# Row-maximum scores of two units written to two neighbouring banks, with one maximum instruction over 1024 columns

## The reference, cut to what matters

```python
scores = jnp.einsum('bhqd,bhkd->bhqk', q, k) * scale + mask
a = jax.nn.softmax(scores, axis=-1)
```

## Time and profile before

| | |
|---|---|
| median of 3 executions | 1685.04 us (1684.78 to 1686.82) |
| the profiled execution's own time | 1684.44 us |
| its span, first to last instruction | 1682.7 us |
| DVE busy | 1244.4 us in 3785 instructions |
| of that, the row maxima (line 881) | 516.8 us in 768 instructions |
| mean granted TensorE clock | 0.96 of full speed |

### The profile page before, as it was taken

How to read it: one execution, slowest core, us unless ns; L and a number is a source line. 1 busy time by engine, 2 the same in 40 slices (tenths; PEclk the granted TensorE clock), 3 DMA queues, 4 the chain that set the end, 5 groups by cost and what they waited for, 6 DMA issues and landing times.

```text
span 1682.7 us, 39867 instructions
## 1 busy us (share of the span) xinstructions
PE 1513.9 (90%) x13672; PEld 1095.7 (65%) x13672; DVE 1244.4 (74%) x3785; ACT 914.0 (54%) x1919; POOL 725.6 (43%) x1097
## 2 busy tenths in 40 slices
PE   5569999999999999999999999999999872999993
PEld 3346776676766767777777777766777552777772
DVE  2346888888888878878888888888887742688883
ACT  1235666666666666666666666666666542222220
POOL 1111444444444444444444444444444333366666
PEclk8789999999999999999999999999999985999997
DMA  4997466766666666666666566666666302355540
GB/s 108 191 201 140 83 106 107 107 104 102 103 100 100 101 103 103 101 101 104 98 104 105 103 105 103 103 104 106 102 97 96 93 27 88 104 163 178 175 133 11
DMA packets 253512, 183.56 MB, mean 109 GB/s; under 512 B 29284, under 2 KB 251943, under 8 KB 253310
## 3 DMA queue, kind: packets, MB, share of 16 engines
q1 hardware_dynamic: 244126, 176.22, 57.5%
q0 software_dynamic: 6912, 3.73, 0.8%
q10 hardware_dynamic: 2272, 1.06, 0.3%
HBM read 55.78 MB, written 38.04 MB: 56 GB/s over the span
## 4 chain that ended last, share of the span: by engine, by line
PE 64%; POOL 11%; DVE 9%; issue 8%; SPq 5%; DMA 1%; ACTq 1%; ACT 1%; POOLq 0%; DVEq 0%
PE bank L1242 13%; PE bank L1389 8%; PE bank L1348 7%; PE bank L1224 4%; SPq L406 4%; PE bank L1232 4%; PE bank L1273 4%; PE bank L1270 3%; PE bank L1211 3%; DVE bst L817 3%; POOL rstd L526 3%; PE bank L1203 3%; PE bank L1199 3%; POOL slots_scratch L581 2%; POOL xrow L592 2%
## 5 line engine op out<-in xcount | busy, mean ns | idle before, releaser
L881 DVE TENSOR_REDUCE mx<-bank 128x2 f32<-128x512 f32 (+1 forms) x768 | 516.8, 674 | 170.3 <-PE bank L1270 90.2
L667 ACT ACTIVATE pt<-bank 128x512 f32<-128x512 f32 x768 | 450.7, 594 | 295.4 <-PE bank L1211 171.0
L1242 PE MATMUL bank<-xnT,weff 128*128 128x256 f32 x1024 | 257.8, 396 | 13.8 <-DVE rest L865 13.1
L1242 PEld LDWEIGHTS bank<-xnT,weff 128*128 128x128 f32 x1024 | 188.7, 194 | 50.2 <-DVE rest L865 15.3
L1273 PE MATMUL bank<-stack 96*128 96x256 bf16 x1024 | 197.7, 275 | 5.6 <-DVE mx L881 5.3
L1211 PE MATMUL bank<-stack 100*128 100x128 bf16 x2048 | 198.8, 219 | 0.0
L548 POOL TENSOR_TENSOR parts<-rest,parts 128x512 bf16<-128x512 f32 x128 | 147.1, 1159 | 115.4 <-ACT parts L684 115.4
L678 ACT ACTIVATE parts<-bank,bqk 128x256 bf16<-128x256 f32 x256 | 107.5, 471 | 136.4 <-PE bank L1242 126.2
L559 POOL TENSOR_TENSOR obuf<-obuf,xrow 128x512 f32<-128x512 f32 x32 | 40.6, 1270 | 326.4 <-ACT obuf L709 326.4
L1211 PEld LDWEIGHTS bank<-stack 100*128 100x128 bf16 x2048 | 158.6, 97 | 12.9
L1208 PE MATMUL bank<-tri,identb 128*128 128x256 bf16 x512 | 141.0, 275 | 20.0 <-DMA stack<-mT 18.2
(11 more groups left out here) (152 smaller groups left out, 2754.9 us busy)
## 6 DMA issues: line engine op xcount, KB each, us to landing
stack<-parts SPq DMA_DIRECT2D x384, 128.0 KB, 5.9
stack<-parts SPq DMA_DIRECT2D x768, 64.0 KB, 2.6
slots_scratch<-zeros SPq DMA_DIRECT2D x5, 2080.0 KB, 12.5
xr<-x SPq DMA_DIRECT2D x32, 256.0 KB, 8.7
out<-obuf SPq DMA_DIRECT2D x32, 256.0 KB, 2.2
ew<-w_gate SPq DMA_DIRECT2D x32, 256.0 KB, 4.0
ew<-w_up SPq DMA_DIRECT2D x32, 256.0 KB, 5.2
ew<-w_down SPq DMA_DIRECT2D x32, 256.0 KB, 4.4
```

The source lines that it names most:

```text
L667: act.activation(pt[:, u % 8, :], S2[u % 2][:, :], ACT.Exp).then_inc(p_ready, 1)
L881: dve.reduce_max(dst, src, AX.X).then_inc(s1_read, 1)
L1242: last = pe.matmul(bank[:, t * WIN:(t + 1) * WIN], weff[:, b, c, qk * D + t * P:qk * D + (t + 1) * P], xnT[:, par, c, :], start=(c == 0), ...
```

## The change

Banks 0 and 1 are declared as one tensor of 1024 columns. PE at every even k now runs `row_scores(k)` and `row_scores(k + 1)` one after the other, and nothing of it at odd k; `s1_full` is raised once, after the second. DVE at every even k takes the maxima of both units (a **duo**) with one `reduce_max` over 1024 columns, and nothing at odd k. `row_scores` of an even unit waits until the duo before has been read; for unit 0 that is the last duo (units 22 and 23) of the step before. Both semaphores count 12 per step (`DUOS`) where they counted 24.

```diff
+    DUOS = UNITS // 2
...
-        banks = [ctx.enter_context(nc.psum_tensor(f"bank{n}", [P, 512], f32)) for n in range(8)]
+        S1 = ctx.enter_context(nc.psum_tensor("bank_pair", [P, 1024], f32))
+        banks = [S1[:, 0:512], S1[:, 512:1024]] + [ctx.enter_context(nc.psum_tensor(f"bank{n}", [P, 512], f32)) for n in range(2, 8)]
...
             def maximum(u, a):
 
-                wait(dve, s1_full, a, UNITS, u)
+                wait(dve, s1_full, a, DUOS, u // 2)
                 if u in (0, LU):
                     wait(dve, maxima_split[u // LU], back(a), 3, 1)
+                view = mx[:, int(u >= LU), :, :].rearrange("p q (h t) -> p t h q", t=2)
                 if u < LU:
-                    dst = mx[:, 0, :, :].rearrange("p q (h t) -> p t h q", t=2)[:, u // 4, (2 * u) % 8:(2 * u) % 8 + 2, :]
-                    src = S1[u % 2][:, :].rearrange("p (h q n) -> p h q n", h=2, q=2)
+                    dst = view[:, u // 4, (2 * u) % 8:(2 * u) % 8 + 4, :]
+                    src = S1[:, :].rearrange("p (h q n) -> p h q n", h=4, q=2)
                 else:
                     h = u - LU
-                    dst = mx[:, 1, :, 2 * (h % 8) + h // 8]
-                    src = S1[u % 2][:, :].rearrange("p (q n) -> p q n", q=2)
+                    dst = view[:, h // 8, h % 8:h % 8 + 2, :]
+                    src = S1[:, :].rearrange("p (h q n) -> p h q n", h=2, q=2)
                 dve.reduce_max(dst, src, AX.X).then_inc(s1_read, 1)
...
-                    wait(dve, s1_read, w, UNITS, (LU, UNITS)[b] - 1)
+                    wait(dve, s1_read, w, DUOS, (LU, UNITS)[b] // 2 - 1)
...
-                    if b:
+                    if b and k % 2 == 0:
                         maximum(k, b)
...
-                if u >= 2:
-                    wait(pe, s1_read, b, UNITS, u - 2)
-                else:
-                    wait(pe, s1_read, back(b), UNITS, UNITS - 2 + u)
-                bank = S1[u % 2]
+                if u % 2 == 0 and u:
+                    wait(pe, s1_read, b, DUOS, u // 2 - 1)
+                elif u == 0:
+                    wait(pe, s1_read, back(b), DUOS, DUOS - 1)
+                bank = banks[u % 2]
...
-                last.then_inc(s1_full, 1)
+                if u % 2:
+                    last.then_inc(s1_full, 1)
...
-                    if b:
+                    if b and k % 2 == 0:
                         row_scores(k, b, 1 - par)
+                        row_scores(k + 1, b, 1 - par)
```

More of the change, by code:

```diff
@@ L171, in attention_moe_program @@
             bst_e = sb("bst_e", [P, NCH, 6], on=experts)
-        banks = [ctx.enter_context(nc.psum_tensor(f"bank{n}", [P, 512], f32)) for n in range(8)]
+        S1 = ctx.enter_context(nc.psum_tensor("bank_pair", [P, 1024], f32))
+        banks = [S1[:, 0:512], S1[:, 512:1024]] + [ctx.enter_context(nc.psum_tensor(f"bank{n}", [P, 512], f32)) for n in range(2, 8)]
         S2, PV, PJ, TR = banks[2:4], banks[4], banks[5:7], banks[7]
-        S1 = banks[0:2]
         w_in = [sem("w_in_l"), sem("w_in_g")]
```

## The result

The changed kernel takes 1733.24 us (median of 4, 1731.17 to 1734.57) against 1684.91 us for the kernel before on the same chip: a ratio of 1.028, 95% interval 1.027 to 1.030. It is slower by 48 us. The forecast was 1738 us, in a range of 1703 to 1762. The profiled execution took 1731.93 us.

A forecast was written before the change was run, and what follows sets the result against it. A step was taken as a loop through PE, DVE, POOL and DVE, 1.24 us longer after the change. Profiled 1684.44 + 36.0 (loop) + 1.0 (earlier steps) + 16.2 (clock falls) = 1737.6, written 1738 us; range 1703 to 1762, own range 1725 to 1757.

The forecast's parts named there:

- The instruction: DVE's row maximum over 1024 columns: estimated to last 1.22 us, 1.14 start to start, against 1.20 for two of 512.
- Rivals 4 and 5: 4: wide reduction cheap, kernel faster, 1673 us, chance 0.08; 5: two passes of 512, 5 us more than forecast.
- Rows moved forward: On PE, row 15 now stands ahead of scores(15), and the duo starts only behind it: +0.22 us a step.
- Behind stats(3): On DVE from stats(3) to row 0, PE now needs the whole duo 22/23, not only maximum(22): +0.54 us.
- The middle: DVE from the duo to moments(0): two duos (2.28 us) where three maxima (1.80 us) lay, +0.48 us.
- Row 0 to row 14: PE's part of the loop: no cost expected; narrowest at the projection at k = 5, 0.3 us left.
- Row 16: PE waits there for duo 14/15, starting 0.75 us later; free while PE's 1.24 us to spare lasts.
- The clock: PE's clock falls to 0.50 behind longer waits at row 0: 10 of 29 steps at 1.62 us, 16.2 us.
- Rival 1: The clock holds: same longer loop, no falls behind row 0, 1721.4 us; chance 0.22.
- Rival 2: The clock falls behind row 0 in every step, 47.0 us in all: 1768.4 us; chance 0.06.
- Rival 3: POOL's own work sets x1 and hides the middle; only the last 0.54 us remain: 1701 us; chance 0.05.
- D: Time of a duo's maximum on DVE, start to start: taken as 1.14 us, bounds 0.60 and 1.20.

The follow-up runs named there:

- e2: Changed kernel with the statistics of the next input and of y moved to position 15 on DVE, both moments ahead of duo 16/17: 1725.08 us.
- e9_order_alone: Kernel before with only PE's order changed: both units' row scores back to back at even k, each keeping its own signal, bank and 512-column maximum: 1796.16 us.
- e3: Changed kernel with PE's four transposes of the next normalised input at position 0 done three times over: 1722.71 us.
- e4_stats_behind: Changed kernel with the statistics of x1 and their moments moved behind the last duo of the step on DVE: 1685.31 us.
- e1_two_reads: Changed kernel with each duo read by two 512-column maximum instructions back to back, one signal behind the second: 1741.27 us.
- e8_odd_duo: Changed kernel with DVE taking each duo at the odd position instead of the even one, PE unchanged: 1890.80 us.

## Why the prediction was right

**The bound.** That a step is one loop through PE, DVE, POOL and DVE is shown: 0.88 us of useless work on PE ahead of row 0 change nothing in it, and taking x1 out of it, with the second loop cut too, takes 1.83 us off the step of the changed kernel (41.27 to 39.44) and 1.39 us off that of the kernel before (40.00 to 38.61).

**The instruction.** Forecast 1.22 us, measured 1.225 (median); start to start 1.14 (670.23 to 671.37). Two reads instead of one cost 0.20 us a step, forecast 0.18. Rivals 4 and 5 fall with this: a duo is far from 0.73 us. That DVE's busy time would fall by some 55 us was a miss: 50 us in the group's sum, 20 us for the engine, since I had taken the sum for both.

**The terms.** Rows moved forward +0.21 (0.22). Behind stats(3) +0.54 (0.54). The middle came out at +0.60, where 0.48 was forecast: the sums of the routing (line 976 to 979) start 0.25 us behind each other where it was 0.13 us with a maximum's work between them. That this is a semaphore's way which maximum(15) had covered is argued from the code, where the second of these instructions waits for the first; it was not tried. The 0.12 us were not in my sum. In exchange 0.06 us went between moments(0) and x1. My reason for this term was too simple, though: e2 shows that three inputs of x1 arrive together, and moments(0) was last by 0.1 us.

**Row 0 to row 14.** Forecast: no change, 0.3 us of cover left at the projection at k = 5. Measured: -0.02 us; rest_part(0) ends at 650.77 and the projection starts at 651.11, 0.34 us later, and PE waits for nothing there.

**Row 16.** Forecast: starts 0.75 us later, a wait of about 0.8 us, at no cost while PE has 1.24 us to spare. Measured 0.74 us; the wait at row 0, forecast at 1.73 us, measured 1.83. The wait at row 16 was free in the changed kernel, and is 21 us of the 23 us that the pairing costs (29 x 0.74) once row 0 no longer hides it.

**The clock.** This is the term that was mis-sized: "I take 10 of 29" falls, 16.2 us; there were six, 9.9 us. The price of one was right, 1.62 us forecast, 1.61 to 1.65 in five of them. The premise behind the count was wrong, so that it came within four was luck. The forecast took a fall to depend on the length of the wait, with an edge near 1.68 us. The runs show no such edge. In the changed kernel a wait of 1.73 us at row 0 had a fall behind it and 23 waits of 1.82 us and more had none. In e9_order_alone 19 of 27 waits of 1.20 us had one, while in the kernel before 26 waits of 1.22 to 1.24 us had none. In the undisturbed part of the changed kernel the falls stand in every sixth step (row 0 at 476.62, 725.85 and 975.12), so the moment seems to count as well; which property decides stays open. e3 shows that falls go when 0.86 us of the wait is filled with work. It cannot tell the shorter wait from the added work. Rival 1, that the clock holds, is refuted here: falls stand behind waits of 1.83 us. By the section "HAM oscillation" of "TensorE: Matmul & The Clock Gate" in the Trainium skill the clock would hold at such waits. The traces disagree: a fall stands also behind waits of 1.20 us in e9_order_alone and behind one of 1.00 us in e4_stats_behind. Rival 2 is refuted by the 23. Rival 3 fell with the row of the middle term.

Two slips in the recorded numbers change nothing in the forecast: 3 falls with D = 1.10 give 1723 us and 20 falls with D = 1.20 give 1759 us, where 1725 and 1757 are written, and the chances outside the whole range add up to a little over 0.2.

The sum: forecast 36.0 + 1.0 + 16.2 = 53.2 us; measured on the profiled executions 47.5 us, of which 35.6 are the loop (28 x 1.27), 9.9 the falls in the steady part, and 2.0 the ends and what the kernel before itself had in irregular steps.

## What to carry to other kernels

Ask of an instruction whether it is on the loop that sets the step, and what stands behind it on its engine: half as many reductions took 50 us off the sum of their times and 20 us off DVE's busy time, and put 48 us on the kernel, because results that the loop needs came later. Two buffers read as one are one buffer: the writer then waits for the whole read, and every place where it had less other work than that read takes is a new wait. And before thinning out an engine, look for the wait in its list that blocks others without need; moving two items by some positions was worth 43 us here, with not one instruction removed.

## What was unexpected on the hardware

A wait of PE of 1.00 us at scores(8) had a fall of the clock behind it in e4_stats_behind (eight matmuls of the output projection took 3.62 us, as behind the 3.03 us wait of the earlier trace rows), and in e9_order_alone most waits of 1.20 us had one, while 23 waits of 1.8 us and more at row 0 of the changed kernel had none. So a wait that is safe in one kernel need not be in another.

In the changed kernel DVE's normalisation at position 14 takes 1.42 us where the same instruction takes 0.42 us at position 20. It was left out of the forecast. Beside it runs POOL's multiplication of y by gamma, and the five kernels in which they meet at different offsets show how the two depend on each other (medians of 23 to 28 steps, in us):

| kernel | DVE begins after POOL's begin by | DVE's duration | POOL's duration |
|---|---|---|---|
| before | 0.32 | 1.24 | 1.28 |
| e1_two_reads | 0.20 | 1.35 | 1.27 |
| after | 0.13 | 1.42 | 1.27 |
| e9_order_alone | 0.03 | 1.52 | 1.27 |
| e8_odd_duo | -0.04 | 0.41 | 1.51 |

Where POOL begins first, DVE's instruction ends 0.28 us behind the end of POOL's, whenever it began: it is held until POOL is done. Where DVE begins first, by 0.04 us, it takes its short time and POOL's instruction is the longer one. From e8_odd_duo, DVE and then POOL:

```profile
548.50 0.41 DVE L923 TENSOR_TENSOR On<-otok,rden 128x256 f32<-128x256 f32 x1
```

```profile
548.54 1.51 POOL L566 TENSOR_TENSOR ybuf<-fbuf,gamma_row 128x512 f32<-128x512 f32 x1 [3.08 <-ACT fbuf L697]
```

So 1.0 us of DVE's time at position 14 hangs on which of the two engines is there first.
